# Grouped attention on Trainium2: Q's loads issued ahead of K's stores, and both rounds with V moved to the end of a slot on TensorE

## The chip, the core and the metric

The kernel runs on one core of one Trainium2 chip. The metric is the device time of one execution in microseconds (us); the time of a kernel is the median of its runs.

## What is computed

A chain of four layers over x of shape (16, 512, 128): differential attention, a layer with grouped attention and a mixture of experts, eight blocks of linear attention, and a feed-forward layer. The change touches only the second layer's attention:

```python
# 16 sequences of 512 tokens, 128 features, 16 heads of 8, 4 heads of K and V
q = (h @ Wq).reshape(b, s, 16, 8)
k = (h @ Wk).reshape(b, s, 4, 8)
v = (h @ Wv).reshape(b, s, 4, 8)
q, k = rope(q), rope(k)            # each K and V head serves 4 heads of Q
scores = einsum('bhqd,bhkd->bhqk', q, k) / sqrt(8)
attn = softmax(where(causal, scores, min))
ctx = einsum('bhqk,bkhd->bqhd', attn, v)
h = clip(residual + ctx @ Wo, -100, 100)   # then router and experts
```

## The kernel before

`grouped_attention` writes out one program for each engine; they meet only through semaphores. The work is cut into **slots**: slot n handles one pair of heads, eight slots make one sequence, so there are 128 slots and sequences b = 0 to 15, with s = 0 to 7 the place in a sequence (n = 8b+s+1, so that sequence b's slots run one place late).

In every slot TensorE (PE) does two things with the same Q and K. `score(n, part)`, part 0 to 2 (L355, with masks L325 in part 0), makes the scores with keys on the partitions, which ScalarE (ACT) turns into probabilities `PT` with `exponentials(n, part)` (L537 and L539 for part 0, L544 and L545 for part 1, L547 for part 2). `max_scores(m, part)` (L379, masks L325) makes scores with queries on the partitions for a pair 11 slots ahead (AHEAD), from which VectorE (DVE) takes maxima in `take_max(m, part)` (L791, L794, L798). In the text S0, S1, S2 are the three parts of `score`, M0, M1, M2 those of `max_scores`. They are issued as S0, M0, S1, (one small job), (a round with V), M1, S2, M2, (another small job), (a round with V). All six write into three pairs of PSUM banks in turn, so that each unit waits for the reader of the unit three places back:

- M1 waits for the exponentials of S0, S2 for the maxima of M0, M2 for the exponentials of S1;
- the next slot's S0 waits for the maxima of M1, its M0 for the exponentials of S2, its S1 for the maxima of M2.

The round with V is `weigh` (L388): four matmuls, one for each of four heads, on 32 columns of the array each. A group of four heads takes two slots: the even slot does key tiles 0 (512 columns) and 2 (256), the odd slot key tiles 1 (384) and 3 (128). Its probabilities are those of two slots earlier; ACT copies its result at the start of the next even slot (`copy_o`, L505), and it is turned by L259. The small jobs use one more bank M: turning the output (L259), projections of a later sequence (L215 to L240), transposes and matmuls of the router (L287 to L310), the output projection (L268, L278). ACT has a copy to make for most of them; in s = 1 (L524) and s = 5 (L498) that copy stands between the exponentials of S0 and those of S1. DVE has a longer piece of other work at the end of most slots: `split_q` in s = 0 (L779 to L783), `split_k` in s = 1, `choose` in s = 2 (which ends with `sel`, L867), `shift` in s = 3.

Q and K of a sequence reach the matmuls by way of DRAM: `store_q` (L1008 to L1012), `store_k` (L1018 to L1020), `load_q` (L1027, waits until Q's stores have landed) and `load_k` (L1034, waits for K's), all issued by SyncE (SP) on one queue. They are first used by M0 of slot s = 4 of the sequence two before it (m a multiple of 8), which waits for both loads.

Of the kernel before, what the change touches and what calls it, by code (L numbers as in the profile page):

```python
# [47 lines left out]
def grouped_attention(nc, C, XT, H, G, T, R, NB):  # L48
# [8 lines left out]
    FIRST = ((0,), (2,))  # L57
    SECOND = ((1,), (3,))
# [5 lines left out]
    with ExitStack() as ctx:  # L64
# [131 lines left out]
        def pe_program(pe):  # L196
# [187 lines left out]
            def weigh(n, tiles):  # L384
                for j in tiles:
                    for c in range(4):
                        at = KEPT[c % 2][j]
                        last = pe.matmul(O[32 * c:32 * c + 32, j * P:SEQ],  # L388
                                         V[(n // 4) % BUF][:, j, n % 4, :],
                                         PT[:, (2 * n + c // 2) % RING, at:at + NT - j, :].rearrange(  # L390
                                             "p a q -> p (a q)"),
                                         start=(j == 0), stop=(j == 3), skip_group_check=True)
                return last
# [13 lines left out]
            for b in range(-1, NB + 1):  # L407
                p, c, c2, c3, r = b - 1, b + 1, b + 2, b + 3, b - 2
                for s in range(8):
                    n = 8 * b + s + 1  # L410
                    m = 8 * b + s + 1 + AHEAD
                    group = 4 * b + s // 2 - 1
                    attending, scanning = 0 <= n < 8 * NB, 0 <= m < 8 * NB and b > -2
                    weighing = 0 <= group < 4 * NB
                    if attending:
                        score(n, 0)
                    if scanning:
                        max_scores(m, 0)
                    if attending:
                        score(n, 1)  # L420
                    if s == 0 and exists(p):
                        turn_o(p, 2)
                    if s == 1 and exists(r):
                        turn_h(r)
                    if s == 2 and exists(p):
                        turn_o(p, 3)
                    if s == 3 and exists(r):
                        rank(r)
                    if s == 4 and exists(b):
                        turn_o(b, 0)  # L430
                    if s == 5 and exists(c):
                        turn_max(c)
                    if s == 6 and exists(b):
                        turn_o(b, 1)
                    if s == 7 and exists(c3):
                        project_qs(c3)
                    if weighing and s % 2 == 0:
                        pe.wait_ge(probs, 6 * group + 6)
                        if group:
                            pe.wait_ge(o_copied, group)  # L440
                        weigh(group, FIRST[0])
                    if weighing and s % 2 == 1:
                        weigh(group, SECOND[0])
                    if scanning:
                        max_scores(m, 1)
                    if attending:
                        score(n, 2)
                    if scanning:
                        max_scores(m, 2)
                    if s == 0 and exists(c2):  # L450
                        sum_k(c2)
                    if s == 1 and exists(r):
                        route(r)
                    if s == 2 and exists(c2):
                        project_v(c2)
                    if s == 3 and exists(p):
                        turn_y(p)
                    if s == 4 and exists(p):
                        project_out(p)
                    if s == 5 and exists(c3):  # L460
                        turn_x(c3)
                    if s == 6 and exists(c3):
                        project_q(c3)
                    if s == 7 and exists(c3):
                        project_kk(c3)
                    if weighing and s % 2 == 0:
                        weigh(group, FIRST[1])
                    if weighing and s % 2 == 1:
                        weigh(group, SECOND[1]).then_inc(av_ready, 1)
# [533 lines left out]
        def sp_program(sp):  # L1003
            def store_q(c):
                sp.wait_ge(q_split, c)
                if c >= 3:
                    sp.wait_ge(q_loaded, 32 * (c - 2))
                sp.dma_start(stq[c % 2, :, 0:3, :], partsQ[:, 0:1, :].to_broadcast([P, 3, SEQ])  # L1008
                             ).then_inc(q_stored, 16)
                sp.dma_start(stq[c % 2, :, 3:5, :], partsQ[:, 1:2, :].to_broadcast([P, 2, SEQ])  # L1010
                             ).then_inc(q_stored, 16)
                sp.dma_start(stq[c % 2, :, 5:6, :], partsQ[:, 2:3, :]).then_inc(q_stored, 16)  # L1012

            def store_k(c):
                sp.wait_ge(k_split, c)
                if c >= 3:
                    sp.wait_ge(k_loaded, 32 * (c - 2))
                sp.dma_start(stk[c % 2, :, 0:3, :], partsK[:, 0:3, :]).then_inc(k_stored, 16)  # L1018
                sp.dma_start(stk[c % 2, :, 3:5, :], partsK[:, 0:2, :]).then_inc(k_stored, 16)
                sp.dma_start(stk[c % 2, :, 5:6, :], partsK[:, 0:1, :]).then_inc(k_stored, 16)  # L1020

            def load_q(c):
                sp.wait_ge(q_stored, 48 * c)
                if c >= BUF:
                    sp.wait_ge(scored, 24 * (c - BUF + 1))
                for e in range(2):
                    sp.dma_start(qT[c % BUF][64 * e:64 * e + KR, :, :],  # L1027
                                 stq[c % 2].rearrange("(p e d) s n -> e (d s) p n", e=2, d=HD)[e]
                                 ).then_inc(q_loaded, 16)

            def load_k(c):
                sp.wait_ge(k_stored, 48 * c)
                for e in range(2):
                    sp.dma_start(kT[c % BUF][64 * e:64 * e + KR, :, :],  # L1034
                                 stk[c % 2].rearrange("(g d) s n -> (d s) g n", d=HD)
                                 ).then_inc(k_loaded, 16)

            def store_max(c):
                sp.wait_ge(mT_copied, c + 1)
                if c >= 2:  # L1040
                    sp.wait_ge(m_loaded, 32 * (c - 1))
                sp.dma_start(stm[c % 2], mT[:, :]).then_inc(m_stored, 16)

            def load_max(c):
                sp.wait_ge(m_stored, 16 * (c + 1))
                for e in range(2):
                    sp.dma_start(qT[c % BUF][64 * e + KR:64 * e + KR + 3, :, :],
                                 stm[c % 2].rearrange("(e j p) n -> e j p n", e=2, j=3)[e]
                                 ).then_inc(m_loaded, 16)

            sp.dma_start(wout[:, :], C["g_wout_dram"]).then_inc(w_loaded, 16)
            sp.dma_start(wr[:, :], C["wr_dram"]).then_inc(w_loaded, 16)
            sp.dma_start(ln2w[:, :], C["ln2w_dram"]).then_inc(w_loaded, 16)
            sp.dma_start(mats[:, :, :], C["route_mats_dram"]).then_inc(w_loaded, 16)
            sp.dma_start(vecs[:, :], C["route_vecs_dram"]).then_inc(w_loaded, 16)
            for e in range(2):
                sp.dma_start(k12[64 * e + KR:64 * e + KR + 3, :, :, :].rearrange("p c g n -> p (c g) n"),
                             G["ones"][:, :].unsqueeze(1).to_broadcast([3, (BUF - 1) * KV, SEQ])
                             ).then_inc(ones_loaded, 16)
            sp.wait_ge(zeroed, 1)  # L1060
            for k in range(SPARE):
                sp.dma_start(rows_of(xs, E * REGION + SEQ * k),
                             blank[:, :].unsqueeze(1).to_broadcast([P, NT, ROW])).then_inc(padded, 16)
            for b in range(-1, NB):
                c, c2 = b + 1, b + 2
                if exists(c2):
                    store_q(c2)
                    store_k(c2)
                    load_q(c2)
                    load_k(c2)  # L1070
                if exists(c):
                    store_max(c)
                    load_max(c)
            sp.wait_ge(plan_ready, 1)
            sp.wait_ge(padded, 16 * SPARE)
# [2793 lines left out]
```

## Time and profile before

| | |
|---|---|
| median of 3 runs | 3165.83 us (3156.24 to 3166.15) |
| the profiled execution: its time, its span | 3165.76 us, 3164.0 us |
| stage of the change, from the first mask of this layer's attention to its last round with V | about 525 to 1267 us |
| TensorE busy, of the span | 2882.8 us (91%) |
| VectorE, ScalarE, GpSimdE busy | 2482.6, 2326.2, 2104.2 us |
| mean granted TensorE clock | 0.954 |

Busy time is that in which an engine had an instruction under way. The chain of work that ended last lies in the last layer and does not reach back to this stage; since the layers follow one another, a microsecond saved or lost here is one in the total.

### The profile page before, as it was taken

The page shows a single profiled execution, that of the slowest core. Times are in us where ns is not written, and L with a number is a line of the kernel's source. Part 1 is how long each engine was busy: PE and PEld are TensorE (multiplying, and loading weights), DVE is VectorE, ACT ScalarE, POOL GpSimd, SP SyncE. Part 2 cuts the span into 40 slices and gives each one's busy share as a digit, 9 for nine tenths or more (in the row PEclk, how much of TensorE's full clock was granted, in tenths as well). Part 3 has the DMA queues.
Part 4 walks back from the last instruction along what each step waited for, and adds up shares of the span by engine and source line. Part 5 has one row for each costly group of instructions (what it writes and reads, how often), then busy time and mean ns, then how long its engine had stood idle before and what let it go on. Part 6 is the DMA issues. An engine that isn't in the chain of part 4 may idle for free. (4 is left out here: it accounts for less than half of the span.)

```text
span 3164.0 us, 66212 instructions
## 1 busy us (share of the span) xinstructions
PE 2882.8 (91%) x22258; PEld 1871.3 (59%) x22258; DVE 2482.6 (78%) x6944; ACT 2326.2 (74%) x3601; POOL 2104.2 (67%) x2402
## 2 busy tenths in 40 slices
PE   6999997788998888789579999999999999999979
PEld 3555554344444444678246666666666666666668
DVE  5777776788888875567468888888888888888867
ACT  5888883466666667444289999999999999999833
POOL 5666673346555543577657888788877888788745
PEclk8999997799999999899789999999999999999989
DMA  4544534223322330685400000000000000000001
GB/s 121 131 108 112 129 92 91 59 62 69 69 57 60 72 70 19 191 271 158 128 1 1 17 1 17 1 7 11 6 12 1 17 1 17 1 17 1 1 14 41
DMA packets 151509, 178.31 MB, mean 56 GB/s; under 512 B 18619, under 2 KB 122784, under 8 KB 151076
## 3 DMA queue, kind: packets, MB, share of 16 engines
q1 hardware_dynamic: 142084, 157.14, 19.2%
q0 software_dynamic: 9088, 16.94, 1.6%
q8 instruction: 179, 2.93, 0.4%
q14 instruction: 158, 1.29, 0.1%
HBM read 99.82 MB, written 75.95 MB: 56 GB/s over the span
## 5 line engine op out<-in xcount | busy, mean ns | idle before, releaser
L3380 PE MATMUL lb_FF<-lb_h,lb_w 128*128 128x512 f32 x1024 | 502.0, 592 | 0.0
L3609 DVE TENSOR_SCALAR lb_z<-lb_M,lb_mv,lb_rstd 128x128 f32<-128x128 f32 x1024 | 344.9, 398 | 3.3 <-POOL lb_rstd L3534 3.0
L3497 ACT ACTIVATE lb_h<-lb_H,lb_prm 128x512 f32<-128x512 f32 x512 | 327.5, 699 | 2.6 <-PE lb_H L3371 2.6
L3534 POOL TENSOR_TENSOR lb_rstd<-lb_rstd,half 128x4 f32<-128x4 f32 x256 | 260.8, 1019 | 37.2 <-issue 1.3
L3365 PE MATMUL lb_H<-lb_x1s,lb_w 128*128 128x512 f32 x512 | 273.0, 533 | 0.0
L3380 PEld LDWEIGHTS lb_FF<-lb_h,lb_w 128*128 128x128 f32 x1024 | 193.5, 189 | 89.9 <-issue 61.1
L3601 DVE BATCH_NORM_STATS2 lb_stats<-lb_M 128x6 f32<-128x128 f32 x1024 | 226.9, 284 | 15.5 <-PE lb_M L3324 9.0
L1649 POOL TENSOR_SCALAR_AFFINE_SELECT da_PT<-da_PT 128x1024 f32<-128x1024 f32 x128 | 149.1, 1165 | 133.4 <-ACT da_PT L1566 133.3
L3366 PE MATMUL lb_H<-lb_x1s,lb_w 128*128 128x512 f32 x512 | 203.3, 397 | 0.0
L3371 PE MATMUL lb_H<-lb_x1s,lb_w 128*128 128x512 f32 x512 | 202.7, 397 | 0.1
L3552 POOL CAST lb_x1s<-lb_x 128x512 fp32r<-128x512 f32 x128 | 78.3, 611 | 173.7 <-DVE lb_x L3634 173.7
L2631 POOL DMA_INDIRECT moe_ys<-moe_y,moe_dest x156 | 159.0, 1019 | 50.5 <-issue 44.9
L794 DVE TENSOR_REDUCE ga_bm<-ga_S 128x8 f32<-128x1024 f32 x128 | 156.5, 1222 | 42.5 <-PE ga_S L379 41.4
L791 DVE TENSOR_REDUCE ga_bm<-ga_S 128x8 f32<-128x1024 f32 x128 | 156.0, 1219 | 42.4 <-PE ga_S L379 41.8
L1571 ACT ACTIVATE da_PT<-da_SY 128x1536 f32<-128x1536 f32 x128 | 184.8, 1443 | 0.0
L1566 ACT ACTIVATE da_PT<-da_SX 128x1024 f32<-128x1024 f32 x128 | 131.0, 1023 | 67.4 <-PE da_SX L1404 67.1
L3545 POOL TENSOR_TENSOR lb_xs<-H,lb_xs 128x512 fp32r<-128x512 f32 x126 | 167.8, 1332 | 18.1
L3555 POOL TENSOR_TENSOR lb_x1s<-lb_x,lb_x1s 128x512 fp32r<-128x512 f32 x128 | 163.5, 1277 | 20.8 <-issue 20.8
L3566 POOL TENSOR_TENSOR lb_y<-lb_ao,H 128x512 f32<-128x512 f32 x128 | 165.4, 1292 | 16.0 <-ACT lb_ao L3484 14.0
L1439 PE MATMUL da_O<-da_PT,da_V 128*32 128x128 f32 (+2 forms) x3584 | 174.6, 335 | 0.0
L3578 POOL TENSOR_TENSOR lb_y<-lb_ff,lb_x 128x512 f32<-128x512 f32 x128 | 165.1, 1290 | 8.5 <-PE lb_M L3324 5.3
L3478 ACT ACT_TABLE_LOAD x131 | 168.1, 1283 | 2.3
(514 smaller groups left out, 8860.8 us busy)
## 6 DMA issues: line engine op xcount, KB each, us to landing
moe_w<-experts_dram SPq DMA_DIRECT2D x39, 384.0 KB, 3.2
da_qT<-da_stq SPq DMA_DIRECT2D x64, 192.0 KB, 4.1
da_kT<-da_stk SPq DMA_DIRECT2D x64, 192.0 KB, 3.8
moe_x<-moe_xs SPq DMA_DIRECT2D x39, 260.0 KB, 3.6
tc_g<-moe_ys SPq DMA_DIRECT2D x32, 256.0 KB, 3.5
ga_q<-ga_stq SPq DMA_DIRECT2D x20, 384.0 KB, 5.8
lb_split<-moe_parts SPq DMA_DIRECT2D x8, 896.0 KB, 6.4
da_stq<-da_parts SPq DMA_DIRECT2D x16, 384.0 KB, 2.4
```

What stands on the lines that cost most here:

```text
L1439: last = pe.matmul(O[32 * c:32 * c + 32, q0:q0 + cols], V[:, (n // 4) % 2, j, 2 * (n % 4) + c % 2, :], PT[:, (2 * n + c // 2) % RING, c % ...
L1571: act.activation(PT[:, n % RING, :, 512:HEAD_COLS], SY[:, :, :].rearrange("p a n -> p (a n)").rearrange("p (i n) -> p i n", i=2), ACT.Exp, ...
L3365: pe.matmul(H[:, k % 2, :], w1[:, 0, k, :], x1s[:, 0, :], start=True, stop=False)
L3366: pe.matmul(H[:, k % 2, :], w1[:, 1, k, :], x1s[:, 0, :], start=False, stop=False)
L3371: pe.matmul(H[:, k % 2, :], w1[:, 0, k, :], x1s[:, 1, :], start=False, stop=True).then_inc(h_filled, 1)
L3380: pe.matmul(FF[:, :], w2[:, k, :], h[:, k, :], start=(k == 0), stop=(k == KC - 1)).then_inc(ff_filled, 1)
L3478: act.preload_act_table_set("gelu_apprx_tanh_and_others")
L3497: act.activation(h[:, k, :], H[:, k % 2, :], ACT.Gelu_apprx_tanh, bias=col(FB1 + k, i)).then_inc(h_ready, 1)
L3534: pool.tensor_tensor(out[:, :], out[:, :], C["half"][:, 0:NT], ALU.pow).then_inc(done, 1)
L3545: pool.tensor_tensor(part_of_x(i, 1), state(i), part_of_x(i, 0).bitcast(F32), ALU.subtract).then_inc(xs_ready, 1)
L3601: v.bn_stats(stats[:, t, :], M[:, t * P:(t + 1) * P])
L3609: last = v.tensor_scalar(z[:, t, :], M[:, t * P:(t + 1) * P], mv[:, t, 0:1], rstd[:, t:t + 1], ALU.subtract, ALU.mult)
```

## The change

SP issues Q's two loads after Q's three stores, ahead of K's three stores. PE issues the slot's first round with V not after S1 and the first small job, but after M2 and the second small job, directly ahead of the second round. Nothing is added or removed; DVE, ACT and GpSimdE (POOL) keep their order.

```diff
@@ pe_program, in the loop over slots
                     if s == 7 and exists(c3):
                         project_qs(c3)
-                    if weighing and s % 2 == 0:
-                        pe.wait_ge(probs, 6 * group + 6)
-                        if group:
-                            pe.wait_ge(o_copied, group)
-                        weigh(group, FIRST[0])
-                    if weighing and s % 2 == 1:
-                        weigh(group, SECOND[0])
                     if scanning:
                         max_scores(m, 1)
...
                     if s == 7 and exists(c3):
                         project_kk(c3)
+                    if weighing and s % 2 == 0:
+                        pe.wait_ge(probs, 6 * group + 6)
+                        if group:
+                            pe.wait_ge(o_copied, group)
+                        weigh(group, FIRST[0])
+                    if weighing and s % 2 == 1:
+                        weigh(group, SECOND[0])
                     if weighing and s % 2 == 0:
                         weigh(group, FIRST[1])
@@ sp_program
                 if exists(c2):
                     store_q(c2)
+                    load_q(c2)
                     store_k(c2)
-                    load_q(c2)
                     load_k(c2)
```

On PE, in a slot s = 0 in the middle of the stage (ga_O takes the result of the round with V, ga_S holds scores, ga_M is the bank of the small jobs), the order before is:

```order
 L259 MATMUL ga_M<-ident,ga_oT 128x128 x4
 L388 MATMUL ga_O<-ga_PT,ga_v 32x512 x4
 L379 MATMUL ga_S<-g_k,g_q 128x384 x2
 L379 MATMUL ga_S<-g_k,g_q 128x128 x2
 L355 MATMUL ga_S<-ga_q,ga_k 128x256 x2
 L379 MATMUL ga_S<-g_k,g_q 128x256 x2
 L233 MATMUL ga_M<-ga_rotK,g_pair_sum 32x512
 L388 MATMUL ga_O<-ga_PT,ga_v 32x256 x4
 L325 MATMUL ga_S<-identb,half_masks 128x4x64 x4
```

And the same slot of the changed kernel:

```order
 L259 MATMUL ga_M<-ident,ga_oT 128x128 x4
 L379 MATMUL ga_S<-g_k,g_q 128x384 x2
 L379 MATMUL ga_S<-g_k,g_q 128x128 x2
 L355 MATMUL ga_S<-ga_q,ga_k 128x256 x2
 L379 MATMUL ga_S<-g_k,g_q 128x256 x2
 L233 MATMUL ga_M<-ga_rotK,g_pair_sum 32x512
 L388 MATMUL ga_O<-ga_PT,ga_v 32x512 x4
 L388 MATMUL ga_O<-ga_PT,ga_v 32x256 x4
 L325 MATMUL ga_S<-identb,half_masks 128x4x64 x4
```

The four matmuls of 512 columns now stand behind M1, S2, M2 and the small job; between S1's neighbour L259 and M1 there is nothing any more. Odd slots change in the same way with their 384 columns.

On SP, one sequence's transfers through DRAM (ga_stq and ga_stk are the DRAM tensors), as a piece of the difference:

```order
 L1010 DMA ga_stq<-ga_partsQ 128x2x512
 L1012 DMA ga_stq<-ga_partsQ 128x512
-L1018 DMA ga_stk<-ga_partsK 32x1536
-L1019 DMA ga_stk<-ga_partsK 32x1024
-L1020 DMA ga_stk<-ga_partsK 32x512
-L1027 DMA ga_q<-ga_stq 48x8x512 x2
+L1027 DMA ga_q<-ga_stq 48x8x512 x2
+L1018 DMA ga_stk<-ga_partsK 32x1536
+L1019 DMA ga_stk<-ga_partsK 32x1024
+L1020 DMA ga_stk<-ga_partsK 32x512
 L1034 DMA ga_k<-ga_stk 48x4x512 x2
```

Q's two loads, with their wait for Q's stores, move past K's three stores.

## Rows read from the trace of the kernel before

**Rows 1.** The page, part 1: busy us, share, instructions.

```profile
PE 2882.8 (91%) x22258; PEld 1871.3 (59%) x22258; DVE 2482.6 (78%) x6944; ACT 2326.2 (74%) x3601; POOL 2104.2 (67%) x2402
```

**Rows 2.** Stretches: length, then busy time by engine, granted clock, DMA share, GB/s.

```profile
627.42:1157.04 529.62, 472.53 (x5841) 244.49 (x5838) 435.68 (x918) 337.29 (x802) 294.98 (x404) 0.95 0.28 64
1025.84:1068.68 42.84, 37.49 (x492) 19.62 (x488) 36.48 (x80) 28.10 (x67) 25.81 (x36) 1.00 0.30 67
1030.72:1036.46 5.74, 4.65 (x68) 2.88 (x65) 4.58 (x8) 3.45 (x8) 2.31 (x2) 1.00 0.16 51
1041.42:1047.23 5.81, 3.90 (x68) 2.24 (x65) 5.18 (x26) 3.77 (x9) 5.02 (x9) 1.00 1.00 162
1047.23:1054.28 7.05, 5.18 (x64) 2.98 (x65) 5.51 (x13) 2.97 (x7) 6.25 (x7) 1.00 0.27 55
813.00:817.00 4.00, 4.00 (x44) 2.49 (x47) 3.24 (x7) 2.83 (x6) 1.53 (x3) 0.57 0.49 165
```

**Rows 3.** Timeline of PE in a slot s = 0: start, us, line, operation.

```profile
802.62 0.39 PE L325 MATMUL ga_S<-identb,half_masks 64*128 64x256 bf16 x4
...
804.42 1.06 PE L388 MATMUL ga_O<-ga_PT,ga_v 128*32 128x512 f32 x8
805.42 0.39 PE L379 MATMUL ga_S<-g_k,g_q 48*128 48x384 bf16 x4
...
805.76 0.27 PE L379 MATMUL ga_S<-g_k,g_q 48*128 48x256 bf16 x2
...
806.94 0.64 PE L388 MATMUL ga_O<-ga_PT,ga_v 128*32 128x256 f32 x8
807.51 0.28 PE L325 MATMUL ga_S<-identb,half_masks 64*128 64x256 bf16 x2
```

**Rows 4.** Timeline of a slot s = 7 near the end, without small jobs.

```profile
1196.59 0.39 PE L325 MATMUL ga_S<-identb,half_masks 64*128 64x256 bf16 x4 [0.62 <-DVE ga_bm L794]
...
1198.96 0.41 ACT L545 ACTIVATE ga_PT<-ga_S 128x256 f32<-128x256 f32 x1
...
1199.43 0.28 PE L379 MATMUL ga_S<-g_k,g_q 48*128 48x256 bf16 x2 [0.17 <-ACT ga_PT L545]
```

**Rows 5.** Timeline of PE in an odd slot s = 1, and M2 of a slot s = 5.

```profile
1204.82 0.39 PE L325 MATMUL ga_S<-identb,half_masks 64*128 64x256 bf16 x4 [0.53 <-DVE ga_bm L794]
...
1208.42 0.28 PE L379 MATMUL ga_S<-g_k,g_q 48*128 48x256 bf16 x2 [0.51 <-ACT ga_PT L545]
...
836.25 0.28 PE L379 MATMUL ga_S<-ga_k,ga_q 48*128 48x256 bf16 x2 [0.48 <-ACT ga_PT L545]
```

**Rows 6.** Waits of PE, 627 to 1157 us: total us, times, longest.

```profile
PE ga_S L325 <- issue: 15.8, 10, 4.5
PE ga_S L355 <- DVE ga_bm L791: 13.6, 13, 1.7
PE ga_M L304 <- DVE g_sel L867: 13.6, 11, 1.7
```

**Rows 7.** Timeline of SP, and of PE's wait for it, at the stage's start.

```profile
553.85 1.93 SPq L1012 DMA_DIRECT2D ga_stq<-ga_partsQ  x1
...
557.29 0.34 SPq L1018 DMA_DIRECT2D ga_stk<-ga_partsK  x1
...
558.61 0.96 SPq L1027 DMA_DIRECT2D ga_q<-ga_stq  x2
...
559.73 0.84 SPq L1034 DMA_DIRECT2D ga_k<-ga_stk  x2
...
568.05 0.61 PE L325 MATMUL ga_S<-identb,half_masks 64*128 64x256 bf16 x4 [8.70 <-DMA ga_k<-ga_stk]
```

**Rows 8.** DMA issues: count, KB each, median us from issue to landing.

```profile
da_kT<-da_stk SPq DMA_DIRECT2D x64, 192.0 KB, 3.8
...
ga_q<-ga_stq SPq DMA_DIRECT2D x20, 384.0 KB, 5.8
...
ga_k<-ga_stk SPq DMA_DIRECT2D x20, 192.0 KB, 7.5
```

## The prediction

> **What bounds the kernel now.** I began with the page's busy shares [rows 1]: TensorE (PE) is under way 91% of the span, the others clearly less. The layers follow one another, so only this stage counts. The windows give its pace: 12 sequences from 627.42 to 1157.04 in 529.62 us, 44.14 us for eight slots, PE busy 472.53 of it, at a mean clock of 0.95 [rows 2]. One sequence that ran wholly at full clock took 42.84 [rows 2]. So PE is the bound with small holes in it, and a change of order pays or costs by what it does to the holes. The waits name them [rows 6]: M0 of slot s = 4 waiting for Q and K from DRAM ("issue", 15.8 us), S2 waiting for DVE's maxima of M0 (13.6), the router's L304 waiting for `sel` from DVE (13.6 in 11 times, 1.24 each). The timelines then show what stands beside each hole.
>
> The reader should see in the slot at 802.62 [rows 3] that nothing waits in it. PE is full for 4.89 us; M2 stands 3.14 after the slot's start. The first round with V (804.42 to 805.42) lies exactly over the time in which ACT works on S0 and S1. In the slot at 1196.59 [rows 4], which has no small jobs, PE arrives at M2 too early and is let go by ACT's L545 (1198.96 + 0.41), 2.84 after the slot's start. That is ACT's own pace: copy or no copy ahead, its exponentials of S0 and S1 end about 2.8 after S0's start, whatever PE does behind S1. M2 cannot stand earlier than 2.84.
>
> **PE's edit.** It removes nothing; it takes away the round that covered ACT's latency and puts it where nothing is waited for. Its size: 512 columns take 1.06 and 256 take 0.64 [rows 3], 0.21 for each 128 columns, so in the middle of a stream the 512-column round costs 0.85, the 384-column one 0.64 (the rest is pipeline that overlaps). What a slot gains is how much earlier M2 stands; what it pays is the round behind M2.
>
> - s = 0, 2, 6 (4.9 long): M2 from 3.14 to 2.84, gain 0.30, pay 0.85: +0.55 each, +1.65. Check by the whole slot: 2.84, then 1.18 from M2 over the small job to the next round (805.76 to 806.94), 0.85, then 0.57 (806.94 to 807.51) is 5.44 against 4.89.
> - s = 7: the round is 384 columns; its M2 stands some 0.25 later than in rows 3 because the small job ahead is a 512-column projection. Gain 0.55, pay 0.64: +0.09.
> - s = 5: M2 already waits 0.48 for ACT, whose copy L498 stands between the exponentials [rows 5]. No gain, pay 0.64: +0.64.
> - s = 1: 5.74 long [rows 2], because S2 waits for DVE, which is held by `split_q`. ACT's copy L524 lets M2 go at 3.60 (1204.82 to 1208.42) [rows 5]; M2 now stands about 4.2 (5.74, less 0.36 for the last round, less 1.18). With M1 and S2 of the slot before earlier and that slot longer, DVE's wait goes and ACT's 3.60 takes over. Gain 0.59, pay 0.64: +0.05.
> - s = 3: 5.81 long [rows 2]. `sel` is the end of DVE's work behind M2's maxima of s = 2. DVE gets those units earlier, and s = 2 ends 0.55 later, so the 1.24 of waiting [rows 6] nearly goes. DVE's own pieces (maxima, `place`, maxima) then let the next S0 go at about 4.8. I take -1.0; the ends are -0.5 and -1.24.
> - s = 4: 7.05 long where the loads are late [rows 2]. From M0 on it is an ordinary even slot: +0.55. Where the loads are in time, `shift` on DVE holds S2 in both kernels and the 0.85 that used to lie in that wait is exposed. I take +0.6.
>
> Sum: 1.65 + 0.09 + 0.64 + 0.05 - 1.0 + 0.6 = +2.0 us for a sequence. Twelve sequences give 24.4; the first and the last one that scan (s = 0 to 3 or the small jobs missing) give 3 together; the last two, without maxima, I put at nothing, since ACT's exponentials bound them and PE has as much work as before. PE's edit: **+27**.
>
> **SP's edit.** K's stores are 192 KB, Q's loads 2 x 384 KB. Before, K's stores are issued at 557.29, Q's loads at 558.61, K's at 559.73, and PE is let go at 568.05 by K's [rows 7]: K is the later of the two. That transfers behind others on this queue wait is to be read from the landings: 192 KB take 3.8 alone and 7.5 behind Q's 768 KB [rows 8]. Now K's stores stand behind those 768 KB, and K's loads cannot be issued until the stores have landed, so the serial part store, landing, load comes after Q instead of beside it. At the stage's start: Q's loads from about 558, landed 5.8 later near 564, K's stores just behind near 565.5, K's loads from 565.5 with 3.8 to 4.9 (the two together): 570.4, against 568.05, +2.4. The other bound is that the stores are not held up: then all bytes move without a pause, Q's loads started 1 to 3 us sooner, and K lands up to 1.1 earlier. In the later sequences the wait at M0 is 15.8/12 = 1.3 on average, PE reaches s = 4 at about the same time as before (+0.55 + 0.05 + 0.55 - 1.0), and `split_q` stands behind M units that come sooner (an estimate: some 1 us, as M2's 0.30 and the longer slot give), which pays for part of the longer chain. I take +0.3 for each of 13 sequences, between -1.1 and +2.4: +4. SP's edit: **+6**.
>
> The Trainium skill ("DMA: Bandwidth & Descriptors", Queues, rings and completion order) states that on each DMA engine the descriptors of one queue are consumed in ring order while a later one may finish its write before an earlier one. By its first half K's stores start only behind Q's loads, as the landings say; by its second half the completion could be sooner, which is the other bound.
>
> **The clock.** After stalls the granted clock falls to half for some 4 us (0.57 over 813 to 817, in the slot behind one of kind s = 1 with its wait) [rows 2], and a slot then takes 1.5 us more; 44.14 against 42.84 is what that and the loads cost now. The change spreads holes of 0.4 to 1.0 us over all slots and removes two of over 1 us. I count no difference, and keep one more or one fewer such stretch a sequence, ±1.5 x 13 = ±20, for the range.
>
> **Sum.** 3165.76 (the profiled execution, which is the median of the runs) + 27 + 6 = 3199.
>
> **The rivals.**
> 1. Slower as above, 68%: 3174 to 3220, likeliest 3199. Its low end is SP's best bound (27 - 14) less a few us, its high end SP's middle with one clock stretch in most sequences.
> 2. The clock falls more, 15%: with a hole before S2 and M2 in every slot, s = 1, 4 and 5 most, one more half-speed stretch in each sequence and some to spare: 3220 to 3235. For it speaks that the moved round is what kept PE busy in just these places; against it that the slot at 1047.23, 7.05 long with some 2 us of waiting for the loads, kept its clock at 1.00 [rows 2]. The Trainium skill ("TensorE: Matmul & The Clock Gate", A second HAM failure mode) says that frequent short idles between groups of matmuls make the clock swing; by that rule this rival would be the likeliest.
> 3. No change to be measured, 12%: DVE and ACT, served earlier, run ahead, so all of S2's and L304's waits go (27.2 us over 12 sequences) and the clock stays full (1.3 a sequence, 16 us). Against my 27 + 6 that leaves 3157 to 3175.
> 4. Faster, 5%: K's stores aren't held up and K and Q land before PE comes, so the 15.8 of rows 6 goes and some of the 8.70 at the start too [rows 7], and PE pays less than 10 us for the moved round: 3166 - 16 - 3 = 3147, up to 3156. It decides when ACT's exponentials of S1 end before 2.3 instead of 2.84, and rows 4 and 5 say they don't.
>
> Under 0.3% (9.5 us) is about what a measurement of this kernel cannot tell from no change. Slower: 68 + 15 and 2 of rival 3's upper edge, 0.85; same 0.10; faster 0.05. The range of 8 in 10 is 3172 to 3226.
>
> **What the profile after would show.** Right: M2's L379 waits for ACT L545 in nearly every slot (today in few), with s = 0 slots near 5.4 and s = 5 near 5.1; L304 hardly waits; s = 3 shorter than 5; K's load issued some 3 to 5 us later after K's stores than now (1.1 after the last of them), and M0 at the stage's start near 570.4. Wrong: if M2 is let go before 2.8, if even slots stay at 4.9, or if K's loads are issued as early as before. The weakest terms are s = 3 and the clock.

## The result, and the profile after

The changed kernel takes 3202.23 us (median of 4 runs, 3182.64 to 3206.41) against 3164.14 (4 runs): ratio 1.0116, 95% interval 1.0094 to 1.0139. It is slower by 38 us; 3199 had been forecast. The profiled execution took 3204.33 us, its span is 3202.6, 38.6 more than before's. The stage of the change, from its first mask to its last round with V, went from 742.1 to 780.8 us, which is the whole difference: 12 sequences in the middle +35.4, the part ahead of them -1.0, the part behind +4.2.

The page's first part and stretches of the changed kernel (length, busy time by engine, granted clock, DMA share, GB/s), to lay beside [rows 1, 2]:

```profile
PE 2902.8 (91%) x22258; PEld 1899.3 (59%) x22258; DVE 2485.7 (78%) x6944; ACT 2324.9 (73%) x3601; POOL 2100.6 (66%) x2402
```

```profile
622.55:1187.54 564.99, 493.08 (x5840) 264.37 (x5837) 438.68 (x918) 337.10 (x802) 294.75 (x405) 0.93 0.24 60
...
858.77:864.23 5.46, 5.10 (x64) 2.23 (x60) 4.09 (x7) 3.76 (x8) 4.17 (x4) 1.00 0.17 52
...
875.52:880.55 5.03, 3.97 (x69) 2.39 (x66) 4.57 (x20) 3.66 (x9) 4.53 (x8) 1.00 0.63 129
880.55:888.66 8.11, 6.79 (x64) 4.04 (x65) 6.04 (x13) 3.18 (x7) 6.55 (x9) 0.79 0.11 27
...
744.00:748.00 4.00, 3.87 (x24) 2.23 (x24) 2.71 (x4) 0.60 (x1) 2.54 (x5) 0.57 0.00 0
```

The first is the 12 sequences: 47.1 us each for 44.1, at a mean clock of 0.93. Then come single slots of kinds s = 0 (5.46 long), s = 3 (5.03) and s = 4 (8.11, at 0.79), and 4 us inside another s = 4 slot at 0.57, mostly at the lower of the clock's two levels, 1.2 GHz. DVE, ACT and POOL did the work of before.

TensorE's timeline in the s = 0 slot at 858.77 shows the edit as it was meant to act ([rows 3] has the same kind of slot before, one sequence earlier):

```profile
858.77 0.39 PE L325 MATMUL ga_S<-identb,half_masks 64*128 64x256 bf16 x4
...
860.57 0.39 PE L379 MATMUL ga_S<-ga_k,ga_q 48*128 48x384 bf16 x4
...
861.14 0.42 ACT L545 ACTIVATE ga_PT<-ga_S 128x256 f32<-128x256 f32 x1
...
861.16 0.28 PE L355 MATMUL ga_S<-g_q,g_k 51*128 51x256 bf16 x2 [0.19 <-DVE ga_bm L791]
...
861.61 0.28 PE L379 MATMUL ga_S<-ga_k,ga_q 48*128 48x256 bf16 x2 [0.17 <-ACT ga_PT L545]
861.82 1.04 PE L233 MATMUL ga_M<-ga_rotK,g_pair_sum 64*32 64x512 f32 x2
...
862.80 1.50 PE L388 MATMUL ga_O<-ga_PT,ga_v 128*32 128x512 f32 x16
...
864.23 0.39 PE L325 MATMUL ga_S<-identb,half_masks 64*128 64x256 bf16 x4
```

M1 now stands 1.80 after the slot's start, where the round stood; before it stood at 2.80. But S2 now waits for DVE's maxima of M0 and M2 for ACT's L545; M2 stands at 2.84 instead of 3.14, and both rounds (862.80 to 864.23) come behind it with nothing to cover. A full slot without holes has become one with two small ones and a longer end. The waits of PE over the 12 sequences (total us, times, longest), against [rows 6]:

```profile
PE ga_S L355 <- DVE ga_bm L791: 29.7, 75, 1.9
PE ga_S L379 <- ACT ga_PT L545: 22.1, 50, 0.9
PE ga_S L325 <- issue: 6.3, 5, 2.8
PE ga_M L304 <- DVE g_sel L867: 5.7, 11, 0.9
PE ga_S L379 <- ACT ga_PT L539: 3.0, 13, 0.5
PE ga_S L325 <- DVE ga_bm L794: 2.3, 10, 0.3
```

In the kernel before, M2's wait for ACT was:

```profile
PE ga_S L379 <- ACT ga_PT L545: 6.3, 14, 0.5
```

The first two together have grown to 51.8 us (they were 13.6 and 6.3, together 19.9), those for the loads and for `sel` have shrunk from 29.4 to 12.0. What grew in one piece is s = 4. Its S2 (a DVE wait of 1.86) in the slot that starts at 739.76:

```profile
742.10 0.63 DVE L811 TENSOR_SCALAR ga_mp<-ga_mx 128x64 bf16<-128x64 f32 x1
...
742.54 1.21 DVE L791 TENSOR_REDUCE ga_bm<-ga_S 128x8 f32<-128x1024 f32 x1
...
743.81 0.28 PE L355 MATMUL ga_S<-g_q,g_k 51*128 51x256 bf16 x2 [1.86 <-DVE ga_bm L791]
...
744.34 2.05 PE L278 MATMUL ga_M<-ga_wout,ga_yT 128*128 128x128 f32 x8
...
746.32 2.21 PE L388 MATMUL ga_O<-ga_PT,g_v 128*32 128x512 f32 x16
```

DVE is in `shift` (L811) and comes to M0's maxima late; the wait used to hold a round with V and is now bare, and the output projection and both rounds behind it run at half clock.

The mean length of each kind of slot over the 12 sequences (start of one slot's first mask to the next), with PE's edit alone (the first experiment) beside it:

| us | s=0 | 1 | 2 | 3 | 4 | 5 | 6 | 7 | sum |
|---|---|---|---|---|---|---|---|---|---|
| before | 4.89 | 5.72 | 6.00 | 5.70 | 7.42 | 4.48 | 4.97 | 4.96 | 44.1 |
| PE's edit alone | 5.46 | 5.97 | 5.98 | 5.14 | 8.01 | 5.21 | 5.54 | 5.13 | 46.4 |
| both edits | 5.46 | 6.11 | 6.08 | 5.12 | 8.34 | 5.26 | 5.59 | 5.13 | 47.1 |

The trace's granted clock, laid over the same slots, gives the time at half clock (us in 12 sequences, by kind of slot), and with it a length at full clock: length less half of the half-clock time. That takes too much off, since a wait doesn't lengthen with the clock, so it is a lower bound, and what is laid to the clock below is an upper one. Each row is one execution. In the layers that no edit touches the traces of this document differ too: 153 to 183 us at half clock, and 2415.6 to 2425.4 us in length. How far the sums below hold over all executions is told behind experiment 12.

| | s=1 | 2 | 3 | 4 | 5, 6 | sum | length | at full clock |
|---|---|---|---|---|---|---|---|---|
| before | 3.7 | 27.0 | 3.0 | 20.9 | 0 | 54.6 | 529.6 | 502.3 |
| PE's edit alone | 8.3 | 19.0 | 2.6 | 29.0 | 2.5 | 61.4 | 557.3 | 526.6 |
| SP's edit alone | 1.1 | 26.2 | 5.0 | 42.8 | 0 | 75.1 | 542.8 | 505.2 |
| both edits | 11.6 | 22.5 | 1.9 | 37.0 | 5.5 | 78.5 | 565.0 | 525.7 |

In s = 0 and s = 7 there is none in any of the four.

### The profile page after: what moved, and what is told of

It reads as the page before. It is cut to its first block and busy times, and to the rows that moved or that the text cites. A ratio compares the mean times of both kernels' runs of the same rounds, so it can differ in the third digit from the quotient of the medians.

```text
span 3202.6 us, 66212 instructions
## 1 busy us (share of the span) xinstructions
PE 2902.8 (91%) x22258; PEld 1899.3 (59%) x22258; DVE 2485.7 (78%) x6944; ACT 2324.9 (73%) x3601; POOL 2100.6 (66%) x2402
## 5 line engine op out<-in xcount | busy, mean ns | idle before, releaser
L791 DVE TENSOR_REDUCE ga_bm<-ga_S 128x8 f32<-128x1024 f32 x128 | 156.5, 1223 | 116.2 <-PE ga_S L379 116.0
L3601 DVE BATCH_NORM_STATS2 lb_stats<-lb_M 128x6 f32<-128x128 f32 x1024 | 227.3, 285 | 16.7 <-PE lb_M L3324 10.2
L1649 POOL TENSOR_SCALAR_AFFINE_SELECT da_PT<-da_PT 128x1024 f32<-128x1024 f32 x128 | 148.2, 1157 | 129.9 <-ACT da_PT L1566 129.8
L537 ACT ACTIVATE ga_PT<-ga_S 128x512 f32<-128x512 f32 x128 | 76.6, 598 | 145.8 <-PE ga_S L355 145.5
```

What stands on the lines that cost most here:

```text
L3601: v.bn_stats(stats[:, t, :], M[:, t * P:(t + 1) * P])
```

## The experiments

All times are medians; the ratio is to the kernel before, measured beside it on the same chip (3162.8 to 3164.3 us).

**1. PE's edit alone.** SP's order as before, both rounds at the slot's end; the diff is to the changed kernel, those below are to the kernel before.

```diff
                     store_q(c2)
-                    load_q(c2)
                     store_k(c2)
+                    load_q(c2)
                     load_k(c2)
```

> PE's edit alone, SP in the order of before. Theory (the moved round took away the cover over ScalarE's two groups of exponentials, and the hole before S2 in s = 4 lets the clock fall): nearly all of the loss of the whole change, 1.008 to 1.012 of before (3190 to 3202 us); slots s = 0 at 5.4 to 5.5, s = 4 at 8 or more. Rival (the two edits share the loss, K's later loads stretching s = 4): 1.004 to 1.006, and s = 4 near 6.7.

3197.4 us, 1.0109 (1.009 to 1.0128). PE's edit carries nearly all. Over the 12 sequences it costs 27.7 us, 24.3 of it at full clock, where 24.4 had been forecast.

**2. SP's edit alone.** PE as before.

> SP's edit alone, PE in the order of before. Theory: K's stores land some 4.9 us after issue instead of 1.7, K's loads are issued about 2.5 us later but then land in some 4 instead of 7.5, so M0 of s = 4 waits about as long as before or up to 1.5 longer: 1.000 to 1.005 (3164 to 3180 us), the start of the stage 1 to 2 us later. Rival (Q's earlier loads free the queue for K): 0.996 to 1.000, M0 of s = 4 earlier than before.

3179.57 us, 1.0051 (1.0032 to 1.0069). Alone it costs half a per cent, at the upper edge of what its theory gave, and on top of PE's edit next to nothing (1.0116 against 1.0109). Its waits over the 12 sequences:

```profile
PE ga_S L325 <- issue: 24.3, 11, 4.8
PE ga_M L304 <- DVE g_sel L867: 13.6, 11, 1.7
PE ga_S L355 <- DVE ga_bm L791: 12.4, 12, 1.7
```

The loads' wait went from 15.8 to 24.3 us, nothing else moved, and half clock in s = 4 doubled (20.9 to 42.8). In the changed kernel PE comes to s = 4 later, and that pays. Counted from Q's first store, over 13 sequences, M0 of s = 4:

| us after Q's first store | before | SP's alone | both edits |
|---|---|---|---|
| slot s = 4 starts | 13.2 | 13.1 | 15.0 |
| K's loads issued | 7.0 | 11.9 | 11.6 |
| M0, where it waits for the loads | 15.2 (11 times) | 15.9 (12) | 16.0 (6) |

**3. All slots but s = 4** and **4. only s = 4.** The first round moved behind M2 in the slots named, SP as before. Of the edit only the place ahead of M1 is shown; behind M2 stands the same round for the other slots.

```diff
-                    if weighing and s % 2 == 0:
+                    if weighing and s % 2 == 0 and s == 4:   # or s != 4
                         ...
                         weigh(group, FIRST[0])
```

> PE's edit in all slots but s = 4, which keeps its first round with V behind S1; SP as before. Theory (s = 4 is where the exposed round and the fallen clock together cost 2.5 us a sequence, 13 sequences): 25 to 33 us faster than PE's edit alone, 1.000 to 1.003 of before. Rival (the clock falls from the holes in all slots, and would fall elsewhere): less than 12 us faster than PE's edit alone, 1.006 or more of before, with a clock stretch in s = 5 or s = 2 in its place.

> Before, with the first round with V moved behind M2 in slots s = 4 alone. Complement of the kernel that moved it in all others. Theory, terms add: the one that moved it in all slots lost 2.31 us a sequence and the one without s = 4 lost 1.26, so s = 4 alone costs 1.05 us a sequence, 13 us, time 1.003 to 1.005 of before, with s = 4 slots of about 8.4 us. Rival, terms don't add: in s = 4 PE arrives early, waits for the loads in both and the moved round only fills behind; then the cost is its 0.6 us a sequence as predicted, 7 us or less, 1.000 to 1.002.

3181.26 us, 1.0051 (1.0034 to 1.0068), and 3180.9 us, 1.0048 (1.0032 to 1.0065). The two parts add up to the whole in time, but not in kind. For experiment 3 neither theory held: it is 16 us faster than PE's edit alone, where one said 25 or more and the other under 12. Without s = 4: +18.5 us at full clock, half-clock time 54.6 to 47.8. In s = 4 alone: +3.6 at full clock, 0.3 a sequence, but half clock from 54.6 to 75.1 us, 62.0 of it in s = 4. So the expected size came, 13.8 us over the 12 sequences, by a cause that neither theory had named: up to 10 of it is the clock.

**5. M1 ahead of the first round**, and S2, M2 behind it: round, M1, S2, M2 becomes M1, round, S2, M2.

```diff
+                    if scanning:
+                        max_scores(m, 1)
                     if weighing and s % 2 == 0:
                         ...
                         weigh(group, FIRST[0])
-                    if scanning:
-                        max_scores(m, 1)
```

> Before, with M1 alone moved ahead of the first round with V (order S1, small job, M1, round, S2, M2, small job, round). Theory (a round does no harm where it covers a wait, and DVE is the one that is late): M1 finds its banks free at 1.80 after the slot's start, DVE gets M1 0.6 to 1.0 us earlier, the wait of the next S0 for DVE L794 goes and s = 3 is shorter; M2 stays at 3.1. 0.990 to 0.998 of before. Rival (PE is the bound in most slots and DVE's lateness comes from GpSimd and from M0, not M1): 0.998 to 1.002.

3175.12 us, 1.0034 (1.0021 to 1.0047): slower, so my theory that this place was better fell. Its stretch and its waits for the loads:

```profile
624.12:1165.51 541.39, 491.68 (x5841) 244.88 (x5838) 437.33 (x918) 338.13 (x802) 295.11 (x404) 0.92 0.27 62
```

```profile
PE ga_S L325 <- issue: 20.0, 12, 4.1
```

DVE's waits shrank (L791 13.6 to 9.4, L304 13.6 to 8.9); PE came to s = 4 sooner and stood there longer (20.0 for 15.8 us), and half clock rose to 81.9 us, 56.9 in s = 4. At full clock the 12 sequences are 1.9 us shorter; the clock took back up to 13.6.

**6. M2 ahead, the first round behind S2.** M1, S2, round, M2: it fills the hole ahead of M2 alone.

> PE's first round with V placed between S2 and M2 (order M1, S2, round, M2, small job, round); SP as before. It keeps the hole before S2 (DVE, 0.4 us in an even slot) and closes that before M2 (ACT). Theory (the change loses the covers of two waits, one of 0.4 for S2 and one of 0.45 for M2 beyond it, in every slot): s = 0 at 5.1 to 5.3, between the 4.9 of before and the 5.46 of after, and M2 waits for ACT L545 only in s = 1 and s = 5; 1.004 to 1.009 of before. Rival (what costs is only that both rounds stand together at the end): 0.998 to 1.002.

3181.69 us, 1.0062 (1.0049 to 1.0075): somewhat under half of the loss of experiment 1 comes back. M2 no longer waits for L545; S2 still waits for DVE 63 times. Most comes back where M2's wait had been long: s = 1 is 5.10 us for 5.98, s = 5 4.54 for 5.21. In s = 0 the slot stays at 5.35 for 5.46: S2 stands at 2.39, let go by DVE, and the round behind it puts M2 at 3.60, where it stood at 3.14 in the kernel before. These 0.46 are what s = 0 is longer than before. And s = 4 grew to 9.39 (the loads' wait is 27.0 us), so the time alone says too little of what the filled hole is worth.

**7. Both rounds together, in the middle**, where the first one stood.

> Both rounds with V together, but in the middle (order small job, round, round, M1, S2, M2, small job); SP as before. Theory (the place and not the pair is what costs): PE has no hole before S2 or M2, s = 0 stays at 4.8 to 5.0, but DVE gets M1 0.4 us later, so that the next S0 waits up to 0.4 for it: 1.000 to 1.007 of before, clearly under PE's edit alone (1.0109). Rival (two rounds in a row are bad wherever they stand): 1.009 or more.

3168.53 us, 1.001 (0.9995 to 1.0024). Standing together costs nothing that can be measured; standing at the slot's end does. (It isn't the same kernel in all: its half-clock time is 92.2 us for 54.6, and its 12 sequences are 6.0 us longer, so at full clock it would be the shorter one, by up to 12.7 us. The even time is the sum of the two.)

**8. SP's edit with K's stores on POOL's queue.** PE as before.

```diff
@@ sp_program
                     store_q(c2)
                     load_q(c2)
-                    store_k(c2)
                     load_k(c2)
@@ pool_program
                         third_k(c2)
+                        store_k(c2)
```

> PE in the order of before. SP issues Q's stores, Q's loads and K's loads; K's three stores are issued by GpSimd behind third_k, so on another queue than Q's loads. Theory (in SP's edit alone K's stores are slow only because they stand behind Q's loads in the same queue): K's stores land in under 3.5 us instead of 4.9, K's loads are issued 1.5 to 3 us earlier than in SP's edit alone, M0 of s = 4 waits less than before (mean start under 1.9 after the slot's start): 0.990 to 0.999 of before. Rival (the stores are slow because the 16 DMA engines are shared with Q's loads, whichever queue they stand in): landing still 4.5 or more, 1.003 to 1.008 of before.

3180.82 us, 1.005 (1.0032 to 1.0067), as SP's edit alone. One sequence of it:

```profile
683.89 0.61 POOL L652 DMA_DIRECT2D ga_stk<-ga_partsK  x1 [0.30 <-POOL ga_partsK L645]
684.50 0.50 POOL L653 DMA_DIRECT2D ga_stk<-ga_partsK  x1
684.99 0.50 POOL L654 DMA_DIRECT2D ga_stk<-ga_partsK  x1
...
```

```profile
684.11 0.85 SPq L1028 DMA_DIRECT2D ga_q<-ga_stq  x2
691.91 0.79 SPq L1035 DMA_DIRECT2D ga_k<-ga_stk  x2
```

```profile
685.60:691.90 6.30, 4.23 (x74) 2.33 (x68) 5.32 (x26) 3.90 (x9) 0.12 (x1) 1.00 0.80 152
```

K's loads go out 6.9 us after the last store's issue here, with the DMA engines 80% busy meanwhile; over 13 sequences it is 5.9 us, against 5.5 on one queue, and counted from Q's first store 11.8 against 11.9. The order on the one queue, which the prediction held to be the cause, is not needed for the delay. The DMA packets from 686.0 to 688.7 (packets, MB, share of the 16 engines) show K's first store, on GpSimd's queue q0, moving among Q's loads on q1:

```profile
q1 hardware_dynamic: 550, 0.55, 97.8%
q0 software_dynamic: 32, 0.10, 12.4%
```

In the mean of 13 sequences the first packet of K's stores starts 7.5 us after Q's first store, for 9.0 in experiment 2, but the last one ends at 11.0 in both, when Q's loads land too (11.2 and 11.3). So a queue of their own lets the stores begin sooner and not end sooner. That they share the 16 engines with Q's 768 KB fits. From issue to first packet it is 2.6 us here and 0.8 in the kernel before; whether that is the sharing or a cost of issuing from GpSimd the run does not settle.

**9. The same with M1 ahead of the first round.**

> K's stores issued by GpSimd, and M1 ahead of the first round with V. Theory (M1 first gave 1.9 us of full-clock time over 12 sequences and lost it again at s = 4, whose loads it did not bring forward, and to the clock): with the loads earlier it is 0.985 to 0.997 of before, and faster than with GpSimd's stores alone. Rival (M1 first costs 0.1 in every slot and wins nothing that lasts): 1 to 4 us slower than GpSimd's stores alone.

3187.08 us, 1.0077 (1.0064 to 1.009). The theory fell, since the loads were not earlier. The two losses add: s = 4 is 10.07 us long.

**10. One of Q's two loads ahead of K's stores.** PE as before.

```diff
                     store_q(c2)
+                    load_q(c2, (0,))
                     store_k(c2)
-                    load_q(c2)
+                    load_q(c2, (1,))
                     load_k(c2)
```

> Before, with one of Q's two loads ahead of K's stores on SP (SP's edit by half; PE as before). Question: does the delay of K's stores grow with the bytes ahead of them? Theory, sharing: K's stores, 1.7 us before and 4.9 behind both of Q's loads (768 KB), take about 3.3 behind one (384 KB), K's loads are issued half as late, M0 of s = 4 starts about 2.3 us after its slot (1.92 before, 2.67 with both), time 1.001 to 1.004 of before. Rival, all or nothing: the delay is that of standing behind any load whose issue waits for Q's stores, so the landing takes 4.5 us or more and the time is 1.004 or more.

3152.73 us, 0.9955 (0.994 to 0.9971): faster than before, which neither theory had. Its first sequence:

```profile
558.74 0.33 SPq L1027 DMA_DIRECT2D ga_q<-ga_stq  x1
559.11 0.47 SPq L1018 DMA_DIRECT2D ga_stk<-ga_partsK  x1
559.63 0.42 SPq L1019 DMA_DIRECT2D ga_stk<-ga_partsK  x1
560.09 0.42 SPq L1020 DMA_DIRECT2D ga_stk<-ga_partsK  x1
560.55 0.43 SPq L1027 DMA_DIRECT2D ga_q<-ga_stq  x1
564.72 0.80 SPq L1034 DMA_DIRECT2D ga_k<-ga_stk  x2
```

From K's last store to K's loads it is 1.6 us before, 4.1 here and 5.5 with both of Q's loads ahead (means of 13). The delay grows with the bytes ahead, though the first half of them brings more than the 3.3 that was expected. But Q's first load goes out 1.7 us sooner (4.2 after Q's first store instead of 5.9; in the kernel before Q's stores have landed by 4.2 as well, but SP first issues K's stores, from 4.6 to 5.4) and K's loads 1.9 sooner than in experiment 2, and M0 of s = 4 comes on average at 14.6 after Q's first store, before 15.3. The loads' wait fell from 15.8 to 11.4 us, half clock from 54.6 to 44.4.

**11. The maxima 10 slots ahead instead of 11**, SP and rounds as before. Q and K from DRAM are first used in s = 5; `shift` moves from s = 3 to s = 4, and in s = 5 two small jobs change places.

```diff
-    AHEAD = 11
+    AHEAD = 10
@@ dve_program
-                    if s == 3 and exists(c):
+                    if s == 4 and exists(c):
                         shift(c)
```

**12. The same with M1 ahead of the first round.**

> Before's SP order and rounds, with the maxima running 10 slots ahead instead of 11. Q and K from DRAM are first used one slot later, by M0 of s = 5, so the 15.8 us of waiting for the loads should go; the shift moves to s = 4, and in s = 5 the small job of the maxima and that of x change places. Theory: the bound at the loads was the cause of s = 4's length (7.4 against 5.0 for an even slot) and of the half clock behind it: slots s = 4 near 5.7, time 0.985 to 0.997 of before. Rival: DVE's shift and the maxima's chain into the bias become the wait instead (less slack between the maxima and their use in the exponentials), slots s = 4 or 5 stay above 6.5 and the time is 1.000 or more.

> The same with M1 ahead of the first round with V, which alone won 1.9 us of full-clock time over twelve sequences but came to the loads sooner and lost more there in half clock. Theory: with the loads out of the way its win shows: 0.2 to 0.5% below the version without it. Rival: the half clock comes from the many short holes that this order makes, not from the loads, and it is the same or slower than the version without it.

3138.44 us, 0.9921 (0.9908 to 0.9933), and 3132.29 us, 0.9908 (0.9893 to 0.9922): both beat the kernel before. Stretch and waits of PE of 11:

```profile
617.72:1127.39 509.67, 457.13 (x5841) 235.82 (x5838) 437.94 (x918) 336.94 (x802) 293.88 (x404) 0.98 0.29 66
```

```profile
PE ga_S L355 <- DVE ga_bm L790: 28.3, 23, 2.2
PE ga_M L304 <- DVE g_sel L866: 13.8, 11, 1.4
```

No wait for the loads is left (M0 of s = 5 comes 17.8 us or more after Q's first store in all but one sequence), s = 4 is 5.00 us long for 7.42, and the clock's mean is 0.98. As the rival said, the wait partly moved: S2 of s = 5 now waits for `shift`, 17.7 us in 12 slots, and s = 5 is 5.58 for 4.48. It is worth it all the same: half-clock time fell from 54.6 to 20.5 us, none of it in s = 4. Of the 20 us that the 12 sequences won in this trace, up to 17 are the clock and 3 or more are at full clock; another 6 come from the part ahead of them. The order of experiment 5, which lost on its own, is 2.2 us shorter in the 12 sequences and 6 in the median here, though the two intervals overlap and the gain is nearer 0.1% than the 0.2 to 0.5% that was expected.

**All executions.** The traces show one execution of each kernel, but the mean granted clock was recorded for every one. Twice the missing share of the clock, times the span, is an execution's time at half clock, over the whole program. Changes of the means, with their standard errors, in us, against the 12 to 17 executions of the kernel before that were measured beside each experiment (for both edits, those beside experiment 1):

| | executions | span | at half clock |
|---|---|---|---|
| both edits | 4 | +34.5 ± 5.5 | +11 ± 12 |
| 1, PE's alone | 6 | +33.8 ± 2.3 | +4 ± 7 |
| 2, SP's alone | 6 | +15.6 ± 2.1 | +25 ± 5 |
| 3, all but s = 4 | 6 | +17.7 ± 2.1 | -10 ± 5 |
| 4, only s = 4 | 4 | +15.3 ± 2.0 | +23 ± 5 |
| 5, M1 first | 12 | +10.2 ± 1.9 | +31 ± 5 |
| 6, M2 ahead | 5 | +18.8 ± 1.6 | +10 ± 7 |
| 7, both in the middle | 10 | +3.6 ± 2.3 | +30 ± 5 |
| 8, K's stores on POOL | 6 | +15.8 ± 2.8 | +20 ± 5 |
| 9, the same, M1 first | 5 | +24.4 ± 1.7 | +45 ± 4 |
| 10, one of Q's loads | 5 | -13.5 ± 2.4 | -11 ± 6 |
| 11, 10 slots ahead | 6 | -25.5 ± 1.4 | -23 ± 4 |
| 12, the same, M1 first | 5 | -30.1 ± 1.8 | -22 ± 5 |

So what the clock did in experiments 2, 4, 5, 7, 8, 9, 11 and 12 is no accident of one trace; half of the last column is the most that it can have cost or given. PE's edit alone shows no clean change of the clock, and its loss is work and waits at full clock.

## Why the prediction was right

Time (3202 for 3199), sign and the main terms held. By its own steps:

**PE's edit, +27.** Shown by experiment 1: 24.3 us at full clock over 12 sequences, for 24.4. By kind of slot, change in length less half of the change in half-clock time, forecast in brackets: s = 0 +0.57 (+0.55), s = 1 +0.06 (+0.05), s = 2 +0.31 (+0.55), s = 3 -0.54 (-1.0), s = 4 +0.25 (+0.6), s = 5 +0.63 (+0.64), s = 6 +0.57 (+0.55), s = 7 +0.17 (+0.09). Five are within 0.1. The term is for the whole stage, though, and over all executions PE's edit costs 33.8 us, some 2 of it by the clock at most: some 7 more than 27. Of that the trace shows one piece, the slots at the end that make no maxima, put at nothing because ACT was held to bound them: they take 49.5 us for 47.0, and 49.1 with both edits. The exactness of the sum is partly luck: s = 3 gave back half of what was forecast (L304's wait fell from 13.6 to 5.7 us, it did not nearly go), and s = 2 and s = 4 lost less; these cancel. Where a kind of slot has half clock (s = 1 to 4), its figure is good to some tenths only.

**What bounds M2.** "M2 cannot stand earlier than 2.84" was the step that everything rests on, and it is what the slots show: 2.84 in s = 0, 6 and 7, and in s = 2 where nothing else is late. Against the signs that it named, s = 3 is 5.12 long and not under 5. The prediction named only M2's wait. S2 has one too (0.19 in the s = 0 slot), since the round had also covered DVE's maxima of M0; it lies ahead of M2's and costs nothing extra as long as M2 waits anyway (in experiment 6, where M2 doesn't, it is what keeps s = 0 long), but in s = 3 and s = 4 it is S2 that ends last, which is one reason why M2 waits in 50 slots of 96 and not in nearly all (s = 0, 1, 5 and 6).

**SP's edit, +6.** On top of PE's edit it is 5 us by the medians (3197.4 and 3202.2; the intervals of the ratios overlap) and 11 by the profiled spans (3191.2 and 3202.6), of which 4 lie outside of this stage; over all executions it is under 1 ± 6. At full clock it is nothing measurable (525.7 for 526.6). The forecast of 6 is neither confirmed nor excluded by that. Its mechanism is as told in that K's loads go out 5.1 us after K's last store and not 1.6 (the prediction's 1.1 is counted from Q's first load), and at the stage's start PE is let go 16.9 us after Q's first store and not 15.2, +1.7 for +2.4:

```profile
553.37 0.85 SPq L1027 DMA_DIRECT2D ga_q<-ga_stq  x2
554.27 0.47 SPq L1018 DMA_DIRECT2D ga_stk<-ga_partsK  x1
...
555.24 0.43 SPq L1020 DMA_DIRECT2D ga_stk<-ga_partsK  x1
561.09 0.80 SPq L1034 DMA_DIRECT2D ga_k<-ga_stk  x2
```

Its assumption about PE failed: "PE reaches s = 4 at about the same time as before" was 1.9 us off, since Q's stores go out earlier in the longer slots. That later arrival hides what experiment 2 shows bare. The cause that the prediction gave, order on the one queue, is not supported by experiment 8. Nor do K's stores wait until Q's loads are over: in the changed kernel their first packets start 8.6 us after Q's first store and their last end at 10.9, together with Q's loads (means of 13).

**The clock, 0.** In the profiled executions half-clock time rose from 54.6 to 78.5 us, up to 12 us of the 35.4, and it makes up for terms that came out smaller: 23.4 at full clock and 12 of clock against a forecast of 28 and 0 for the same stretch. But that execution has the lowest clock of the changed kernel's four (0.950; the others 0.952, 0.952 and 0.958). Over all executions the clock's part is at most 6 ± 6 us of 34.5, so the term was off by little or nothing, well within its ±20. The change did take one hole of over 1 us away (L304), but it made the one in s = 4 bare and longer.

**The rivals.** No change and faster are excluded by the interval. The second, one more half-clock stretch a sequence, is at most a part of the truth: in the profiled execution the size came to at most 1.0 us a sequence for the 1.5 that it assumed, and over all executions to less. The Trainium skill ("TensorE: Matmul & The Clock Gate", A second HAM failure mode) puts such swings down to frequent short idles between groups of matmuls. In this case it holds by half at most. The two small holes that the edit put into each slot s = 0, 0.2 us each, brought no half clock at all, and in experiment 6, with S2's hole in most slots, all 51.2 us of it lie in s = 4; 59.5 of the 78.5 us lie in s = 2 and s = 4, as 47.9 of 54.6 did before. But s = 1, whose M2 now waits 0.8 us each time, went from 3.7 to 11.6.

Experiments 3 to 7 name what costs: not that the rounds stand together (7: nothing), not the place of M1 (5), but that nothing covers the waits between S1 and M2. The order before, and that of experiment 5, cover both of them in most slots, DVE's for S2 and ACT's for M2; the order of 6 covers only ACT's and gives back somewhat under half.

## What to carry to other kernels

Work that depends on nothing is cover: put it where the engine would wait for another engine's latency, and cost a move by what the place it leaves was hiding, slot by slot. When PE gets faster ahead of a fixed arrival, as the loads here, it only waits longer, and here such waits also brought half clock behind them; so move the need for the data first (10 slots ahead instead of 11 gave 0.8%), and then an order that lost before seems to pay. If a small transfer gates the next step, don't put all of a large one ahead of it, nor behind it: half and half was the best of the three here.

## What had not been expected of the hardware

How much of the time at half clock hangs on one slot. In s = 4 it was, over 12 sequences: with the loads in time (experiment 11) none, one of Q's loads ahead (10) 17.1 us, before 20.9, both edits 37.0, SP's alone 42.8, both rounds in the middle (7) 43.3, M1 first (5) 56.9, s = 4 alone (4) 62.0. These are one execution each. It is not the loads alone: with both edits PE waits only 6.3 us for them, and 14.3 in s = 4 for DVE ahead of S2. So a stall can cost more than its length: SP's edit alone lengthened PE's waits by some 8.5 us and the 12 sequences by 13.1.

K's 192 KB of stores, 1.6 us from the last issue to the next load's when ahead of Q's 768 KB, took 5.5 behind them on the same queue, and 5.9 on another queue (means of 13 sequences). The Trainium skill ("DMA: Bandwidth & Descriptors", Queues, rings and completion order) says that each DMA engine takes turns between the queues that have work. The run agrees as far as the beginning goes: on their own queue the stores' first packets start at 7.5 us instead of 9.0, among those of Q's loads. It shows no earlier end (11.0 in both), and what holds the last of them is open.
